# A gated mixture-of-experts attention kernel: two experts' gates spread by TensorE from a diagonal, weight splitting in three turns, and steps of group 1 moved later in the first pass

## The reference

```
x = x + tanh(g_xattn) * cross_attention(context, layernorm(x), Wk, Wq, Wv)
x = x + tanh(g_ffn)   * moe_attention(layernorm(x))

moe_attention(h):            # 16 experts
  xn = h / |h|;  sn = sim_matrix / |sim_matrix|
  logits = xn @ sn - sigmoid(gates)
  w = softmax over the experts with logits > 0 (or the best two, if none is)
  q = sum_e w[:, e] * (h @ q_proj[e])      # the same for k and v
  o = softmax(q k^T / sqrt(128)) v         # within a sequence
  out = sum_e w[:, e] * (o @ o_proj[e])
```

## Time and profile before

| | |
|---|---|
| median of three runs | 800.27 us (799.54 to 800.44) |
| the profiled execution | 799.99 us, span 798.1 us, mean granted TensorE clock 0.987 |
| TensorE busy | 776.1 us (97%) |
| VectorE busy | 607.2 us (76%) |
| GpSimd busy | 483.0 us (61%) |
| ScalarE busy | 433.8 us (54%) |

### The profile page before, as it was taken

The page is one execution under the profiler, slowest core; times in us unless marked ns, Lnnn a source line. Parts: engine busy times, 40 slices in busy tenths (PEclk is TensorE's granted clock), DMA queues, the critical chain, the costliest instruction groups (busy, mean ns, idle before and its releaser), DMA issues.

```text
span 798.1 us, 13995 instructions
## 1 busy us (share of the span) xinstructions
PE 776.1 (97%) x3999; PEld 418.1 (52%) x3999; DVE 607.2 (76%) x2037; ACT 433.8 (54%) x1129; POOL 483.0 (61%) x703
## 2 busy tenths in 40 slices
PE   7489999999999999999999999999999999999998
PEld 6445545555455555545555554555555455544444
DVE  2977787878787787778777787877878786775648
ACT  5554645556555655655565565456556555544445
POOL 3276657674746757474675747567574755765534
PEclk9789999999999999999999999999999999999999
DMA  6564476563655636365563636546364654543100
GB/s 192 136 216 159 162 219 174 169 209 94 209 161 164 189 106 204 97 210 167 151 191 106 202 109 209 166 150 186 101 207 116 208 160 139 163 135 116 53 14 28
DMA packets 97476, 122.57 MB, mean 154 GB/s; under 512 B 14611, under 2 KB 69111, under 8 KB 97399
## 3 DMA queue, kind: packets, MB, share of 16 engines
q1 hardware_dynamic: 96679, 121.59, 49.6%
q10 hardware_dynamic: 720, 0.08, 0.1%
HBM read 97.32 MB, written 24.31 MB: 152 GB/s over the span
## 4 chain that ended last, share of the span: by engine, by line
PE 88%; DVE 5%; DMA 2%; POOL 1%; ACT 1%; issue 1%; SPq 0%; DVEq 0%; ACTq 0%; POOLq 0%
PE acc_q L1380 20%; PE acc_k L1380 20%; PE acc_v L1380 20%; PE y L1409 9%; PE oT_p L1409 9%; PE m L1489 2%; PE m L1553 2%; DVE x_all L1175 1%; PE oT_p L1641 1%; PE m L1480 1%; PE m L1539 1%; DMA stage<-in_L_ffn_q_proj_dram 1%; PE m L1469 1%; POOL zq L658 1%; PE m L1529 1%
## 5 line engine op out<-in xcount | busy, mean ns | idle before, releaser
L658 POOL TENSOR_TENSOR zq<-zq_full,zq 128x512 f16<-128x512 f32 x256 | 297.8, 1170 | 222.4 <-ACT zq L743 222.2
L743 ACT ACTIVATE zq<-zq_full 128x512 f16<-128x512 f32 x256 | 160.1, 636 | 224.1 <-DVE zq_full L1145 224.0
L1175 DVE SCALAR_TENSOR_TENSOR x_all<-y,w_out,x_all 128x128 f32<-128x128 f32 x356 | 122.2, 343 | 96.1 <-issue 69.5
L1380 PE MATMUL acc_q<-zq,w_hi 128*128 128x512 f16 x510 | 193.3, 379 | 1.0 <-POOL zq L658 1.0
L1380 PE MATMUL acc_k<-zq,w_hi 128*128 128x512 f16 x510 | 193.2, 379 | 0.0
L1380 PE MATMUL acc_v<-zq,w_hi 128*128 128x512 f16 x510 | 193.2, 379 | 0.0
L1145 DVE TENSOR_TENSOR zq_full<-wq_bc,x2T_p 128x512 f32<-128x512 f32 x256 | 167.8, 668 | 2.5 <-DMA wq_bc<-w_rows 1.7
L1175 DVE SCALAR_TENSOR_TENSOR x_all<-oT_p,w_out,x_all 128x128 f32<-128x128 f32 x356 | 121.5, 341 | 0.0
L673 POOL TENSOR_TENSOR x_all<-stage,x_all 128x128 f32<-128x128 f32 x240 | 100.4, 456 | 19.8 <-DVE x_all L1175 13.3
L1380 PE MATMUL acc_q<-zq,w_lo 128*128 128x512 f16 x255 | 96.6, 379 | 0.0
L1380 PE MATMUL acc_v<-zq,w_lo 128*128 128x512 f16 x255 | 96.6, 379 | 0.0
(11 more groups left out here) (253 smaller groups left out, 1091.4 us busy)
## 6 DMA issues: line engine op xcount, KB each, us to landing
wq_bc<-w_rows SPq DMA_DIRECT2D x128, 512.0 KB, 4.5
blk_rows<-stage SPq DMA_DIRECT2D x26, 256.0 KB, 2.7
stage<-blk_rows SPq DMA_DIRECT2D x104, 64.0 KB, 2.0
blk_rows<-v_blk SPq DMA_DIRECT2D x15, 256.0 KB, 2.0
v_mix<-blk_rows SPq DMA_DIRECT2D x60, 64.0 KB, 2.9
blk_rows<-pc_blk SPq DMA_DIRECT2D x15, 256.0 KB, 4.1
pcT<-blk_rows SPq DMA_DIRECT2D x60, 64.0 KB, 2.0
out_dram<-x_all SPq DMA_DIRECT2D x15, 256.0 KB, 6.7
```

The lines of the kernel that those rows point to most:

```text
L658: nc.gpsimd.tensor_tensor(zq[:, 1, e % Z_SLOTS, :], zq_full[:, e % F_SLOTS, :], zq[:, 0, e % Z_SLOTS, :], ALU.subtract).then_inc(zq_lo_poo ...
L743: nc.scalar.activation(zq[:, 0, e % Z_SLOTS, :], zq_full[:, e % F_SLOTS, :], ACT.Copy).then_inc(zq_hi_done, 1)
L1175: nc.vector.scalar_tensor_tensor(out=rows(x_all, g, b0 + b), in0=bank[:, tok(j)], scalar=w_out[:, g % 2, e, b0 + b:b0 + b + 1], in1=rows(x ...
L1380: last = nc.tensor.matmul(acc[m][:], w[:, m, s, :], zq[:, half, s % Z_SLOTS, :], start=(s == 0 and n == 0), stop=(s == E - 1 and n == 2))
```

## The change

Seven things are done together.

1. **Gates of the experts 0 and 1 of group 0** no longer wait for DRAM. VectorE writes identity times gate (`gate_diagonal`, 128x512, into the unused slot 0 of `wq_bc`), TensorE multiplies with ones (`gate_spread`, a float32 matmul of 128x512 into `m0` and `oT_p`), and `zq_scale` multiplies that PSUM bank with `x2T` in SBUF. The DMA for this slot is not issued; the other slots' DMAs stay.
2. **Weights in three turns**: experts 0 to 3, 4 to 9 and 10 to 15. Three instructions of 128x512 and six of 128x768 take the place of three of 128x2048, on ScalarE and on VectorE each. The last turn stands in the steps 1 to 4 of pass 0. `first_expert` does its three high matmuls ahead of the three low ones.
3. **Head's DMAs**: q_proj goes ahead of the context of the groups 1 to 3, and x of group 1 ahead of v_proj.
4. **Head's order**: `px_transpose(0)` stands behind one context transpose instead of three, and the keys and values of the groups 1 to 3 come after `att_product(0)`; on VectorE `first_stats(1)`, the gates of group 0 and `x_max(1)` stand ahead of `weight_scales(0)`. More dummy matmuls (`keep_busy` 2, 1 and 4).
5. **Later in pass 0**: `att_product(1)` after the first expert, `x1_add(1)` and `second_stats(1)` in step 1, `first_stats(2)` and `second_rstd(1)` in step 2, `second_norm(1)`, `first_rstd(2)` and `x2_norm(1)` in step 3, `x_norm(2)` in step 4; `late(0)` = 3, so that x2^T and the gates of group 1 come two steps later.
6. **o_proj's preparation** one or two steps later: `MAX_AT` (0,4), `SHARE_AT` (0,5) and (0,8), `HIGH_AT` (0,10), `LOW_AT` (0,12).
7. **o^T of group 0** in pass 1 is copied ahead of that step's `zq_high`.

```diff
+BY_PE = 2
+PARTS = ((0, 4), (4, 10), (10, 16))
+GATES_LATE = 3
@@ late(i)
-            return 1 if i == 0 else 0
+            return GATES_LATE if i == 0 else 0
@@
-        MAX_AT, SHARE_AT = (0, 2), ((0, 4), (0, 7))
-        HIGH_AT = (0, 9)
-        LOW_AT = (0, 11)
+        MAX_AT, SHARE_AT = (0, 4), ((0, 5), (0, 8))
+        HIGH_AT = (0, 10)
+        LOW_AT = (0, 12)
@@ SyncE, head
                 sp.wait_ge(kq_in, 16 * 2)
+                load_weights(Q, q_proj)
                 sp.dma_start(zq_full[0:S, 0:PRE]...
-                load_weights(Q, q_proj)
                 load_weights(K, k_proj)
+                load_x(1)
                 load_weights(V, v_proj)
-                load_x(1)
...
-                for j in range(W_SLOTS):
+                for j in range(BY_PE // 2, W_SLOTS):
                     spread_q(0, j)
@@ GpSimd
-                for e in range(LEAD - 1):
+                for e in range(LEAD):
                     zq_low(0, e)
-                second_rstd(1)
-                zq_low(0, LEAD - 1)
-                first_rstd(2)
...
+                    if i == 0 and s == 2:
+                        second_rstd(1)
                     for g, e in zq_at(i, s):
                         zq_low(g, e)
-                    if s == 1 and i < 2:
+                    if s == (3 if i == 0 else 1) and i < 2:
                         second_norm(g2)
+                    if i == 0 and s == 3:
+                        first_rstd(2)
@@ ScalarE, body
+                    if i == 1 and s == Y_FIRST:
+                        oT_high(0)
                     for g, e in zq_at(i, s):
                         zq_high(g, e)
...
-                    if s == (3 if i == 0 else 0) and has(g1):
+                    if s == (4 if i == 0 else 0) and has(g1):
                         x_norm(g1)
+                    if i == 0 and s == 3:
+                        x2_norm(1)
+                    if i == 0 and s in (1, 2, 3):
+                        weight_high((Q, K, V)[s - 1], 2)
@@ VectorE
+            def gate_diagonal(e):
+                wait(dve, w_ready, 1)
+                nc.vector.tensor_tensor(wq_bc[:, 0, e].rearrange("p (b t) -> p b t", b=G),
+                                        ident[:].unsqueeze(1).broadcast_to([P, G, P]),
+                                        w_new[:, 0, e].unsqueeze(2).broadcast_to([P, G, P]),
+                                        ALU.mult).then_inc(w_diag_done, 1)
@@ zq_scale
+                if g == 0 and e < BY_PE:
+                    wait(dve, x2T_sb, 1)
+                    wait(dve, w_spread_ps, e + 1)
+                    nc.vector.tensor_tensor(zq_full[:, e, :], SPREAD_BANKS[e][:], x2T[:],
+                                            ALU.mult).then_inc(zq_full_done, 1)
+                    return
@@ VectorE, head (new order)
 weight_max(K), first_stats(1), setup_gate, x2_norm_inverse(0), weight_max(V), gate_logits(0),
 share_largest(0), gate_mask(0), x_max(1), gate_softmax(0), gate_diagonal(0), weight_scales(0),
 gate_diagonal(1), x_sum(1), zq_scale(0, 0), weight_low(Q), zq_scale(0, 1), weight_low(K),
 weight_low(V), weight_low(Q, 1), zq_scale(0, 2), zq_scale(0, 3), weight_low(K, 1)
@@ VectorE, body
+                    if i == 0 and s == 0:
+                        weight_low(V, 1)
+                    if i == 0 and s == 1:
+                        x1_add(1)
+                        second_stats(1)
+                    if i == 0 and s == 2:
+                        first_stats(2)
+                    if i == 0 and s in (2, 3, 4):
+                        weight_low((Q, K, V)[s - 2], 2)
@@ TensorE
+            def gate_spread(e):
+                pe.wait_ge(w_diag_done, e + 1)
+                pe.wait_ge(logit_read, 1)
+                nc.tensor.matmul(SPREAD_BANKS[e][:], ones[:], wq_bc[:, 0, e], start=True,
+                                 stop=True).then_inc(w_spread_ps, 1)
...
+                keep_busy(4)
+                gate_spread(0)
                 px_transpose(1)
-                att_product(1)
+                gate_spread(1)
@@ TensorE, body
+                    if i == 0 and s == 0:
+                        att_product(1)
```

More of the change, by code:

```diff
@@ L411, in vx_bank, with split_part @@
             return (acc[V], oT_p, acc[K])[g - 1] if 1 <= g <= PRE else m0
+        SPREAD_BANKS = (m0, oT_p)
+        def split_part(t, m, part):
+            experts = slice(*PARTS[part]) if m < O else slice(0, E)
+            return t[:, m, experts].rearrange("p e h -> p (e h)")
         def ctx_slot(g):
@@ L889, in head @@
                 vx_out(0)
-                ctxT_out(1)
                 pxT_out(0)
[L892 to L896, removed]
+                for g in range(1, PRE + 1):
+                    ctxT_out(g)
+                for g in range(1, PRE):
                     kxT_out(g)
@@ L904, in head @@
                 xnT_out(1)
-                x2T_move(0)
+                x_exps(1)
+                weight_high(Q)
                 weight_high(K)
-                x_exps(1)
+                zq_high(0, 0)
+                weight_high(V)
                 pxT_out(1)
-                weight_high(V)
-                for e in range(LEAD):
-                    zq_high(0, e)
+                zq_high(0, 1)
+                weight_high(Q, 1)
+                weight_high(K, 1)
+                zq_high(0, 2)
+                weight_high(V, 1)
+                zq_high(0, 3)
             def body(i):
@@ L971, in body @@
                         kxT_out(g1)
-                    if s == Y_FIRST and has(gc):
-                        wait(act, oT_ps, gc + 1)
-                        wait(act, y_ps, PAIRS_Y * (gc - 1))
-                        nc.scalar.activation(oT[:, gc % 2, 0, :], oT_p[:], ACT.Copy).then_inc(oT_hi_done, 1)
+                    if s == Y_FIRST and i > 1 and has(gc):
+                        oT_high(gc)
                     if s == 10 - sooner(i) and has(g1):
@@ L1237, in head @@
                 weight_max(K)
+                first_stats(1)
                 setup_gate()
+                x2_norm_inverse(0)
                 weight_max(V)
+                gate_logits(0)
                 share_largest(0)
-                first_stats(1)
+                gate_mask(0)
+                x_max(1)
+                gate_softmax(0)
+                gate_diagonal(0)
                 weight_scales(0)
-                x2_norm_inverse(0)
-                gate_logits(0)
-                gate_mask(0)
-                gate_softmax(0)
-                weight_low(Q)
-                x_max(1)
-                weight_low(K)
+                gate_diagonal(1)
                 x_sum(1)
                 zq_scale(0, 0)
+                weight_low(Q)
                 zq_scale(0, 1)
+                weight_low(K)
                 weight_low(V)
+                weight_low(Q, 1)
                 zq_scale(0, 2)
-                x1_add(1)
-                second_stats(1)
                 zq_scale(0, 3)
-                first_stats(2)
+                weight_low(K, 1)
             def body(i):
@@ L1376, in experts @@
                 for m in (Q, K, V):
+                    for part, (first, _) in enumerate(PARTS):
+                        if (i, s) == (0, first):
+                            pe.wait_ge(hi_done[m], part + 1)
+                            pe.wait_ge(lo_done[m], part + 1)
                     if s == 0:
@@ L1498, in x2_transpose @@
                     wait(pe, xnT_sb, g + 1)
+                    wait(pe, zq_full_done, 1)
                 for b in range(G):
@@ L1506, in xn_transpose @@
                     wait(pe, kxT_sb, 2)
-                wait(pe, logit_read, cap(g))
+                if g == 2:
+                    wait(pe, x1_done, 2)
                 for b in range(G):
-                    last = nc.tensor.transpose((acc[Q] if g == 1 else m0)[:, tok(b)], xn[:, b, :], ident[:])
+                    last = nc.tensor.transpose((m0, acc[Q], m1)[g][:, tok(b)], xn[:, b, :], ident[:])
                 last.then_inc(xnT_ps, 1)
@@ L1574, in head @@
                 vx_product(0)
-                for g in range(1, PRE + 1):
-                    ctx_transpose(g)
-                px_transpose(0)
-                kx_product(1)
-                att_product(0)
-                vx_product(1)
-                for g in range(2, PRE + 1):
+                ctx_transpose(1)
+                px_transpose(0)
+                for g in range(2, PRE + 1):
+                    ctx_transpose(g)
+                att_product(0)
+                for g in range(1, PRE + 1):
                     kx_product(g)
```

44 lines of the change are left out of this document (28 added, 16 removed).

## The result

The changed kernel takes 806.69 us (median of four runs, 806.54 to 807.33); the kernel before, beside it, 800.36. The ratio is 1.0082 (95% interval 1.0065 to 1.0100): slower by 6.3 us, where the prediction said 798.5 and 795.4 to 801.3. The profiled execution of the changed kernel took 806.54 us, with a span of 804.8, 6.7 more than before.

The account below looks back on a forecast made before the run. TensorE's work plus its stalls was taken as the bound. 0.4 (pass 0) + 1.2 (o^T) = 1.6 us off 799.99 gave 798.4, as median 798.7; with o^T's upper bound and low half 798.5 was taken, range 795.4 to 801.3.

Parts of the forecast that it names:

- t3: Pass 0: the time when expert 7 ends on TensorE; forecast 63.0 us, against 63.4 before.
- DMA order: Head: q_proj lands at 14.9 us and the context at 15.4, so x1_add(0) starts at 18.5 against 19.02.
- VectorE to the gates: Head: VectorE's queue from x1_add(0) takes 12.6 us, to 31.1; the diagonal is there at 34.9 or 33.4.
- Spreading: Head: each float32 128x512 matmul takes 0.9 us, 1.8 at low clock; two end 2.4 to 4.8 after the diagonal.
- t1: Head: the time when zq_scale(0, 1) starts; forecast 38.4 us, bounds 35.8 and 39.3, against 42.0 before.
- What is given back: Pass 0, t1 to t2: 8.9 us of VectorE work plus 1.8 for meetings (splits and low halves shutting each other out).
- t2: Pass 0: the time when second_stats(1) ends on VectorE; forecast 49.1 us, against 47.9 before.
- The end of the chain: Pass 0: x_norm(2) and its transposes let expert 7 start at 60.3 us; weight_max(O) with gather_max ends a little sooner.
- TensorE keeps what it has: After pass 0's middle: group 1's gates come up to 3 us later, other engines lead by 1.7 to 2, nothing lost.
- o^T: Pass 1: copying ahead of zq_high takes away 1.0 to 1.3 us of TensorE's wait; 1.2 taken.
- Slower: Rival, pass 0: VectorE and GpSimd lock each other out; costs from t3 = 64.6, 801.1 to 802.1 us; chance 0.14.
- Clock up early: Rival, head and pass 0: early clock rise, few meetings, t3 60.2 to 61.9, kernel 795.9 to 797.6 us; chance 0.27.

Follow-up runs that it names:

- e2: The kernel before with one edit alone, q_proj loaded ahead of the context: 803.61 us, ratio 1.0040 to the kernel before.
- e4: The changed kernel with o_proj's gather and spread in steps 7 and 9 and its high split in step 11: 807.03 us, ratio 1.0088.
- e8: e5 with group 1's steps taken one or two steps forward and the transposes of group 2's norm one step later: 803.84 us, ratio 1.0043.
- e1: The changed kernel with the context of groups 1 to 3 loaded ahead of q_proj again: 805.09 us, ratio 1.0055.
- e3: The kernel before with the copy of o^T of group 0 ahead of that step's zq_high, alone: 799.23 us, ratio 0.9983.
- e6: e1 without VectorE's low splits of the second and third weight turns (four-column copies instead, GpSimd zeroing in the head): 801.97 us, ratio 1.0021.
- e10: e8 with x_norm(2) in step 5, behind the copy of x2^T on ScalarE, and first_rstd(2) in step 3: 802.35 us, ratio 1.0024.
- e5: e1 with o_proj's gather and spread in steps 7 and 9 and its high split in step 11: 804.98 us, ratio 1.0058.
- e11: e1 with 28 dummy 128x128 matmuls on TensorE in place of the wait on wmax, ahead of o_proj's gather_max: 804.19 us, ratio 1.0045.

## Why the prediction was wrong

The forecast had an earlier start, given back in the chain through group 1's norms to expert 7. An earlier start there was, of 0.85, and it was given back, and much more, ahead of expert 7. But the head was 4.0 late against the forecast, the wait that ended last ahead of expert 7 was not the norms' but that on `weight_max(O)`, with expert 6 behind it, and a part that it put at nothing cost 1.9. At t3 the measured time is 6.1 later than the forecast.

*DMA order: the step that failed first.* The prediction bounded the context's landing by 16.5, q_proj's landing of before "with the same bytes ahead", and took 15.4. It came at 17.29 (16.60 in e2, 16.92 in e4). The bound counted bytes only, and the bytes were the same; but the issue began 1.0 later than in the kernel before and held SyncE for 2.13 us where it had been 0.31. That is 1.9 of the 3.3 by which `x1_add(0)` was late (21.77 for 18.5; the bounds were 17.6 to 19.6). The rest is the chain from that transpose to `x1_add(0)`: priced at 3.2 from times at the full clock, it took 4.48, because TensorE's clock was 0.50. No term had that. In all three profiled executions with the context behind q_proj (the changed kernel, e2, e4) the clock was 0.50 at `att_product(0)`; of those with the context first, e8's alone had that. With e1's order it took 3.37, and `x1_add(0)` starts at 18.95, near the forecast's 18.5. e2 gives the price of both in the kernel before: 3.2 us.

*VectorE to the gates.* From `x1_add(0)` to the end of the first diagonal: 37.41 + 0.65 - 21.77 = 16.3, against 34.9 - 18.5 = 16.4 forecast (with the low clock). Right.

*Spreading.* 0.9 or 1.8 were the estimates. The first ran at the low clock: its record is 2.08, and 39.98 - 38.11 = 1.87 passed to the next instruction; the second, in which the clock rose, 42.11 - 40.83 = 1.28. From the diagonal (38.06) to t1 (42.41) are 4.35, of the 4.4 of the upper bound; the taken value was 3.5, so 0.8 more. The rise of the clock came, but during the second spread, not before.

*t1* = 42.41 against 38.4: 3.2 from the context and the low clock behind it, 0.8 from the clock in the spreads. Beyond the upper bound of 39.3.

*What is given back, t1 to t2:* 53.2 - 42.4 = 10.8 against 8.9 + 1.8 = 10.7. The sum is right, but partly by luck. The meetings took 0.9 of the 1.8 set for them: 0.6 in the split at 44.62 and 0.3 in one at 48.90. The splits by themselves took 0.70 and 0.93 each, where the prediction had 0.57 and 0.83 (its own rule, 2.35 x 768/2048, gives 0.88, and the fixed starts that it names are not in the 8.9), and a wait for ScalarE took 0.2. *From t2 to the end of `first_rstd(2)`:* 62.44 - 53.16 = 9.3 against 7.8 + 1.2 = 9.0: right. The Trainium skill ("SBUF — State Buffer", the section on the two separate sides) says that the shared port pair is held for the whole instruction; the low halves of 1.60 and 1.67 agree. By its rule the power from 59.23 would have held the split of 59.49 back until 60.27, and the split would have ended near 61.3, by my estimate; it ended at 60.5. The measurement decides: that power was in no meeting.

*The end of the chain: second step that failed.* By the forecast, expert 7 would start 2.2 after `first_rstd(2)`; it started 4.2 after. The prediction wrote that `weight_max(O)`, "57 to 59", with `gather_max` ahead of expert 6 "ends a little sooner than this chain". By its own numbers this was not so: 59, 0.2 of `gather_max` and the 1.94 of expert 6 make 61.1, and the transposes were set at 59.75. It left out that expert 6 stands between the two. Here `weight_max(O)` ended at 62.7, held up last by a split that waited 1.08 for its high half, which stood behind `x2_norm(1)` on ScalarE. Then came expert 6, at the low clock, which no term had: 3.24 instead of 1.94. So t3 = 69.1: 4.0 from t1, 0.4 from the chain, 2.0 here, less 0.2 in expert 7's own time, 6.2 (63.0 was forecast; the tenth is rounding).

*"TensorE keeps what it has": third step that failed.* From t3 to group 1's first expert another 1.9 were lost (5.7 late, then 7.6). Group 1's gates left VectorE at 75.21, and `zq_scale(1, 0)` waited 4.30 for their DMA, to 83.68; before, that was at 75.77. 7.9 later is beyond any lead of 1.7 to 2. On ScalarE `pxT_out` stood behind that expert's `zq_high`, so TensorE waited 1.15 for `pxT` and then 0.45 for the first low half. The prediction had allowed the gates to be "up to 3 later", already more than the lead that was to cover it; they were 8.4 later than in the kernel before (66.81), because their products stand in expert 7, behind everything above.

*o^T.* 1.2 was right: e3 measured 1.2, and in the changed kernel TensorE's wait fell by 1.0.

*The sum.* 6.1 at t3, 1.9 behind it, 0.3 at o^T: 8.3 off a forecast of -1.6, which is the span's +6.7.

*The rivals.* "Slower" named t3 = 64.6 as the point from which the change costs, and 69.1 lies far past it, and past the 66.4 of its own far end. Its sign was right, its cause only in part: leaving out the late splits' work takes 3.1 us away (e6) and still leaves the kernel 1.9 slower than the one before. The DMA order (1.6 in the medians of e1, whose interval overlaps; 3.2 in e2, clear of noise) and the order of group 1's steps (2.6 without touching a split, e10 against e5) are causes that it didn't name. The three prices overlap and need not add up. "Clock up early" didn't happen. The range's lower end, 795.4, was said to leave out that rival's far end, but lies below it (795.9). What would show it was named rightly: `x1_add(0)` after 19.6, a wait on `wmax` before expert 7, a stall between 64 and 100.

*Left open.* e6 leaves out the low splits' work; what it costs to divide them in three turns rather than two or one was not run by itself, and neither was the spread alone in the kernel before. Why the context's issue is held behind q_proj is not known. Why the 256 KB write took 4.9 in e1 and 3.1 in the changed kernel is not known.

## What to carry to other kernels

A DMA that is moved behind a large one can land later than the bytes ahead of it explain, and its issue can hold the queue (0.31 against 2.04 us here): look at who stands behind its reader, and at what clock that work will run after the wait, before trading a 2 us gain for it. When a start is pulled forward, add up the chain that refills the stream behind it to the instruction, with every piece of TensorE's own work that lies between two of the waits; two chains that end within a microsecond of each other are both the bound, and moving one shows the other. A part that can be taken out alone should be: o^T's copy alone is 1.2 us faster than before, and with the other six it is 6.3 slower.

## What the runs showed of the hardware

This stall was paid twice: after TensorE's 3.42 us without work the granted clock was 0.53 from 62 to 64 us and 0.50 from 64 to 65, and nine matmuls of 128x512 took 3.24 us instead of 1.94. Dummy matmuls over the same stretch kept it at 1.00 (e11). The Trainium skill ("TensorE: Matmul & The Clock Gate", Part 1) says that an idle TensorE falls back to 1.2 GHz; these rows agree. In the head the clock of both kernels was 0.50 from 12 us on. In the kernel before, which had no wait there, it was 1.00 again from 15.5; in the changed kernel, with the wait of 2.52, it was 0.50 to 24.

A float32 matmul of 128x512 takes 1.87 us from start to start at the low clock, 1.28 where the clock rose in it, and 0.96 at a granted clock of 1.00 (e8, 35.52 to 36.48).
